# Attention degrees spread over the partitions by DMA instead of by TensorE, with the clears dealt out and every engine's order rewritten

## The reference, cut to what matters

```python
attn = softmax(causal(q @ k.T))                 # per head, 256 x 256
out  = attn @ v
adj  = clip(attn + eye(n), 0, 1)
deg  = adj.sum(-1, keepdims=True)
for l in range(2):
    h = feats @ gnn_w[l] + gnn_b[l]
    feats = gelu((adj @ h) / deg + feats)        # feats starts as v
out  = layer_norm((out + feats @ lin_w + lin_b) @ Wo)
```

## Time and profile before

| | us |
|---|---|
| median of 3 runs (lowest, highest) | 1038.27 (1037.43, 1043.19) |
| the profiled execution | 1036.57 |
| its span | 1034.8 |
| PE, PEld, DVE, ACT, POOL busy | 1010.2, 870.6, 823.1, 780.6, 504.1 |
| batches 0 to 15 on PE | about 12 to 862 |

### The profile page before, as it was taken

The page is one execution under the profiler, slowest core; times in us unless marked ns, Lnnn a source line. Parts: engine busy times, 40 slices in busy tenths (PEclk is TensorE's granted clock), DMA queues, the critical chain, the costliest instruction groups (busy, mean ns, idle before and its releaser), DMA issues.

```text
span 1034.8 us, 27841 instructions
## 1 busy us (share of the span) xinstructions
PE 1010.2 (98%) x8600; PEld 870.6 (84%) x8600; DVE 823.1 (80%) x3622; ACT 780.6 (75%) x2180; POOL 504.1 (49%) x668
## 2 busy tenths in 40 slices
PE   4999999999999999999999999999999999999997
PEld 3788888888888888888888888888888888999995
DVE  4858788888888888888888888898989796767554
ACT  3868787878787878787878787878787876656662
POOL 4524345454545454545464646454545452655443
PEclk9999999999999999999999999999999999999999
DMA  6991000000000000000000000000000021222227
GB/s 170 396 365 36 9 2 16 5 11 8 10 9 10 9 10 9 10 9 10 9 10 9 10 9 10 9 10 9 10 9 10 2 82 44 75 63 73 61 67 253
DMA packets 48964, 50.03 MB, mean 48 GB/s; under 512 B 20601, under 2 KB 39291, under 8 KB 48912
## 3 DMA queue, kind: packets, MB, share of 16 engines
q1 hardware_dynamic: 44592, 40.91, 12.9%
q0 software_dynamic: 4320, 8.47, 2.4%
HBM read 21.23 MB, written 28.58 MB: 48 GB/s over the span
## 4 chain that ended last, share of the span: by engine, by line
PE 92%; ACT 3%; SPq 2%; DMA 1%; DVE 1%; issue 1%; POOL 0%; POOLq 0%; DVEq 0%
PE bank L671 74%; PE bank L748 3%; PE bank L783 3%; PE bank L758 3%; PE bank L761 3%; PE bank L759 3%; PE bank L1040 2%; PE bank L1022 1%; PE bank L989 1%; ACT eb L1174 1%; DMA pairs<-zout,zin 1%; ACT ea L1174 0%; SPq L371 0%; DMA got<-pairs 0%; ACT gt L1144 0%
## 5 line engine op out<-in xcount | busy, mean ns | idle before, releaser
L1478 DVE TENSOR_REDUCE nmax<-bank 128x1 f32<-128x128 f32 (+1 forms) x512 | 148.1, 347 | 25.2 <-PE bank L671 25.2
L535 POOL TENSOR_TENSOR ea<-ea,wgt 128x256 f32<-128x256 f32 x128 | 78.6, 614 | 144.3 <-DVE wgt L1500 144.2
L544 POOL TENSOR_TENSOR deg<-den,rs 128x256 f32<-128x256 f32 x128 | 80.8, 636 | 123.3 <-DVE eb L1491 122.3
L537 POOL TENSOR_TENSOR eb<-eb,wgt 128x512 f32<-128x512 f32 x128 | 133.3, 1041 | 0.0
L1174 ACT ACTIVATE ea<-bank,nmax 128x128 f32<-128x128 f32 x256 | 97.9, 383 | 46.3 <-DVE nmax L1478 35.8
L1174 ACT ACTIVATE eb<-bank,nmax 128x256 f32<-128x256 f32 x256 | 125.8, 491 | 0.0
L1144 ACT ACTIVATE gt<-bank 128x512 f32<-128x512 f32 (+1 forms) x256 | 111.5, 490 | 15.1 <-PE bank L761 10.8
L1491 DVE SCALAR_TENSOR_TENSOR eb<-idw,ssum,eb 128x256 f32<-128x256 f32 x256 | 114.0, 481 | 0.0
L671 PE MATMUL bank<-qk 64*128 64x256 f32 (+1 forms) x1024 | 109.9, 341 | 0.0
L568 POOL DMA_INDIRECT pairs<-zout,zin x71 | 70.8, 997 | 78.7 <-DVE zout L1994 67.4
L671 PE MATMUL bank<-gt,vnat 128*64 128x256 f32 (+1 forms) x1024 | 101.1, 334 | 0.0
(11 more groups left out here) (241 smaller groups left out, 3025.8 us busy)
## 6 DMA issues: line engine op xcount, KB each, us to landing
slots<-gu_lo SPq DMA_DIRECT2D x33, 520.0 KB, 15.0
zin<-slots SPq DMA_DIRECT2D x71, 65.0 KB, 1.8
got<-pairs SPq DMA_DIRECT2D x8, 512.0 KB, 6.4
zin<-in_guT SPq DMA_DIRECT2D x14, 216.0 KB, 2.9
raw_gu<-in_guT SPq DMA_DIRECT2D x8, 352.0 KB, 3.0
out<-x_all SPq DMA_DIRECT2D x7, 256.0 KB, 3.5
pairs<-zout,zin POOLq DMA_INDIRECT x71, 2.4
dn<-in_downT SPq DMA_DIRECT2D x2, 512.0 KB, 15.5
```

Source lines behind the costliest of these rows:

```text
L535: nc.gpsimd.tensor_tensor(ea[:, s], ea[:, s], wgt[:, s, 0:2].unsqueeze(2).to_broadcast([P, 2, P]), ALU.mult)
L537: nc.gpsimd.tensor_tensor(eb[:, s], eb[:, s], wgt[:, s, 2:4].unsqueeze(2).to_broadcast([P, 2, 2 * P]), ALU.mult).then_inc(p_g.sem, 1)
L544: nc.gpsimd.tensor_tensor(deg[:, s], den[:, s, :].unsqueeze(2).to_broadcast([P, 4, DHEAD]), rs[:, s, :].unsqueeze(2).to_broadcast([P, 4, D ...
L1478: done = V.tensor_reduce(nmax[:, n % 3, i:i + 1], score_bank(n, a)[:, TILE_SCORES[t]], X, ALU.max, negate=True)
```

## The change

Degrees go over the partitions by way of DRAM: POOL writes 4 numbers per partition, SP writes them to a DRAM tensor degs as 2 x 256 in the order of tokens, waits for that write (w_kept), and reads them back with each head's row repeated on 64 partitions into deg_wide (4 slots), which raises w_deg.

```diff
-        deg = at("deg", [P, 3, 4, DHEAD])
+        deg = at("deg", [P, 3, 4])
+        deg_wide = at("deg_wide", [P, SPREADS, TOKENS])
...
-        s_deg = Signal(sem("s_deg"), PAIRS)
+        w_kept = [Signal(sem(f"w_kept{i}"), 16 * PAIRS // SPREADS) for i in range(SPREADS)]
+        w_deg = [Signal(sem(f"w_deg{i}"), 16 * PAIRS // SPREADS) for i in range(SPREADS)]
...
 
         def score_bank(n, a):
             return bank[SCORE_BANKS[n][a]][:, :]
@@ -387,10 +392,29 @@
 
 
             sp.wait_ge(k_consts, 1)
-            for r in range(0, SLOT_ROWS, CLEAR * P):
+            def clear(r):
                 sp.dma_start(slots[r:r + CLEAR * P, :].rearrange("(p r) d -> p (r d)", p=P),
                              zero[:, :]).then_inc(w_clear, 16)
 
+            def spread(b, n):
+                i = n % SPREADS
+                p_deg.wait(sp, b, n + 1)
+                sp.dma_start(degs[i].rearrange("a (t p) -> p (a t)", p=P), deg[:, n % 3, :],
+                             allow_slow_non_contiguous=True).then_inc(w_kept[i].sem, 16)
+                w_kept[i].wait(sp, b, 16 * (n // SPREADS + 1))
...
+                sp.dma_start(deg_wide[:, i, :],
+                             degs[i].unsqueeze(1).to_broadcast([2, DHEAD, TOKENS])).then_inc(w_deg[i].sem, 16)
+
+            to_clear = list(range(0, SLOT_ROWS, CLEAR * P))
+
+            def spread_and_clear(b, n):
+                spread(b, n)
+                now = CLEARS * (b * PAIRS + n)
+                for r in to_clear[now:now + CLEARS]:
+                    clear(r)
+
+            for n in range(PAIRS):
+                spread_and_clear(0, n)
 
             sp.wait_ge(k_low, 2)
             sp.wait_ge(k_vlow, 2)
@@ -406,9 +430,18 @@
                     w_part.sem, 16)
 
             part_load(1)
+            for n in range(PAIRS):
+                spread_and_clear(1, n)
+            for r in to_clear[2 * CLEARS * PAIRS:]:
...
+                clear(r)
             with sp.Fori(2, BATCHES - 1) as b:
-                p_low.wait(sp, b - 1, 0)
-                part_load(b)
+                for n in range(PAIRS):
+                    if n == PART_AT:
+                        p_low.wait(sp, b - 1, 0)
+                        part_load(b)
+                    spread(b, n)
+            for n in range(PAIRS):
+                spread(BATCHES - 1, n)
             for e in range(2, EXPERTS):
...
             def degrees(b, n):
 
                 s = n % 3
-                nc.gpsimd.tensor_tensor(deg[:, s], den[:, s, :].unsqueeze(2).to_broadcast([P, 4, DHEAD]),
-                                        rs[:, s, :].unsqueeze(2).to_broadcast([P, 4, DHEAD]),
+                nc.gpsimd.tensor_tensor(deg[:, s, :].rearrange("p (a t) -> p t a", t=TILES),
+                                        den[:, s, :].rearrange("p (t a) -> p t a", t=TILES),
+                                        rs[:, s, :].rearrange("p (t a) -> p t a", t=TILES),
                                         ALU.mult).then_inc(p_deg.sem, 1)
 
             def token_power(p, i):
...
             def attended(b, n):
 
                 d_d.wait(dve, b, n + 1)
-                V.tensor_tensor(aT[:, n, :], psum(DEG_AT[n], TOKENS), aT[:, n, :], ALU.mult).then_inc(d_a.sem, 1)
+                w_deg[n % SPREADS].wait(dve, b, 16 * (n // SPREADS + 1))
+                V.tensor_tensor(aT[:, n, :], deg_wide[:, n % SPREADS, :], aT[:, n, :], ALU.mult).then_inc(d_a.sem, 1)
```

PE's degrees and the table DEG_AT go, and ACT's mixed_values waits for d_d (the difference) instead of d_a. Waits on d_a come into POOL's order, ahead of degrees 3 to 7:

```diff
-                if routed is not None:
-                    a_qk.wait(pool, b, 2)
-                    gate_up_low(b - 1)
                 if after is not None:
                     deviation(b + 1, 0, 3)
-                d_e.wait(pool, b, 1)
+                if routed is not None:
+                    gate_up_low(b - 1)
+                graph(b, 0)
                 degrees(b, 0)
-                graph(b, 0)
                 graph(b, 1)
                 degrees(b, 1)
-                d_e.wait(pool, b, 3)
-                degrees(b, 2)
                 graph(b, 2)
-                d_e.wait(pool, b, 4)
-                degrees(b, 3)
-                graph(b, 3)
-                graph(b, 4)
-                graph(b, 5)
-                degrees(b, 4)
-                graph(b, 6)
-                degrees(b, 5)
                 if after is not None:
                     deviation(b + 1, 1, 7)
-                degrees(b, 6)
-                d_e.wait(pool, b, 8)
-                s_deg.wait(pool, b, 5)
-                degrees(b, 7)
-                graph(b, 7)
+                degrees(b, 2)
+                graph(b, 3)
+                d_a.wait(pool, b, 1)
+                degrees(b, 3)
+                graph(b, 4)
+                d_a.wait(pool, b, 2)
+                degrees(b, 4)
+                d_a.wait(pool, b, 3)
+                degrees(b, 5)
+                graph(b, 5)
+                graph(b, 6)
                 if before is not None:
                     token_power(b - 1, 0)
+                d_a.wait(pool, b, 4)
+                degrees(b, 6)
+                graph(b, 7)
+                d_a.wait(pool, b, 5)
+                degrees(b, 7)
                 if routed is not None:
-                    d_ch.wait(pool, b - 2, 11)
                     scatters(b - 2)
                 if before is not None:
                     token_power(b - 1, 1)
```

In scores the mask products of pairs 1, 3 and 6 (MASKS_LAST) come after the products of queries and keys instead of before them:

```diff
+                masks_last = n in MASKS_LAST
+
+                if not masks_last:
+                    masks()
                 for t in (1, 0):
                     for a in range(2):
                         rows = slice(a * DHEAD, (a + 1) * DHEAD)
                         mm = product(score_bank(n, a)[:, TILE_SCORES[t]], q[rows, xt(t)], k[rows, 0:(t + 1) * P],
-                                     False, True, skip_group_check=True)
+                                     masks_last and t == 1, not masks_last, skip_group_check=True)
+                if masks_last:
+                    mm = masks()
                 mm.then_inc(s_s.sem, 1)
```

More of the change, by code:

```diff
@@ L923, in batch @@
-                if before is None:
-                    folded_rest()
+                scores(b, 7)
+                layer2(b, 0)
+                differences(b, 4)
                 transposes(b, 5)
-                d_z1.wait(pe, b, 1)
-                degrees(b, 4)
-                if routed is not None:
-                    a_exp.wait(pe, b, 16)
-                    places(b - 2, psum(PLACES_AT, PLACES))
-                a_vt.wait(pe, b, 3)
-                layer1(b, 1)
-                if before is not None:
-                    output_natural(b - 1, psum(Y_NOW_AT, TOKENS))
+                if after is not None:
+                    a_exp.wait(pe, b, 15)
+                    queries_keys(b + 1, 0)
+                    d_z2.wait(pe, b, 1)
+                    values(b + 1, 0)
@@ L980, in batch @@
                 layer2(b, 3)
-                if before is not None and after is not None:
-                    a_qk.wait(pe, b + 1, 2)
                 if before is not None:
                     tokens_transposed(b - 1, psum(Z_T_AT, TOKENS))
+                output_graph(b, 0)
             def tokens_transposed(p, o):
@@ L1582, in batch @@
-                a_vt.wait(dve, b, 2)
-                difference(b, 2)
-                attended(b, 2)
-                maxima(b, 6, 0)
-                weights(b, 5)
-                maxima(b, 6, 1)
-                maxima(b, 7, 0)
-                difference(b, 3)
-                maxima(b, 7, 1)
-                attended(b, 3)
-                adjacency(b, 6)
-                weights(b, 6)
+                adjacency(b, 4)
+                difference(b, 2)
+                p_deg.wait(dve, b, 3)
@@ L1594, in batch @@
+                adjacency(b, 5)
+                if before is not None:
+                    output_bias(b - 1)
+                weights(b, 4)
+                attended(b, 1)
+                if before is None:
+                    folded_values()
+                difference(b, 3)
+                weights(b, 5)
                 layer1_out(b, 0)
                 if before is not None:
-                    output_bias(b - 1)
-                p_deg.wait(dve, b, 5)
-                adjacency(b, 7)
@@ L1610, in batch @@
                 if before is not None:
                     norm_tokens(b - 1, 0)
-                attended(b, 5)
-                if routed is not None:
-                    place_tokens(b - 2, 0)
+                layer1_out(b, 1)
+                p_deg.wait(dve, b, 4)
+                adjacency(b, 6)
+                attended(b, 2)
+                weights(b, 6)
+                attended(b, 3)
+                maxima(b, 7, 0)
+                maxima(b, 7, 1)
                 if before is not None:
@@ L1651, in batch @@
                     norm_tokens(b - 1, 8)
+                attended(b, 6)
+                if before is not None:
                     norm_tokens(b - 1, 9)
```

384 lines of the change are left out of this document (183 added, 201 removed).

## The result

The changed kernel takes 1729.95 us (median of 6 runs, 1727.47 to 1732.73) against 1038.41 (1036.56 to 1043.19): 1.666 times as long, 95% interval 1.664 to 1.669. The forecast was 1021. Its profiled span is 1725.7 us.

The account below looks back on a forecast made before the run. PE alone was taken to bound each batch: 16 batches x (1.6 - 0.3) = 20.8 us, less 6 at the end, 14.8 off 1036.57 gives 1021.8, called 1021; its own range 1011 to 1028, 8 in 10 1009 to 1034.

Parts of the forecast that it names:

- The sign: Whole kernel: forecast faster, with chance 0.77; within 0.5% 0.10, slower 0.15.
- The spread's time: Each pair's degree write to DRAM and read back: 3.9 to 5.9 us, taken as 5, hidden behind 8 us of DVE's order.
- the far row of 15: Spread's transfers: a queued transfer of 15 us, named as the other far row beside the 5 us taken.
- SP does not bound: SP's queue in each batch: held for 8 x 2.9 = 23 of 50.7 us plus its issues.
- Rival B: Loop: spread late, kernel slower; each microsecond over the cover of 8 paid twice per batch; 1054 at 9 us; 12%.
- the ring: Loop's cycle attended(n), degrees(n+3), write, read, attended(n+3): turns twice in a batch, with a cover of 8 us.
- The clears at 0: Batches 0 and 1: 33 writes of 520 KB, dealt out two behind each pair, costed at 0.
- PE's work and the new order: PE in each batch: 52.32 - 1.74 for removed transposes + 0.15 for the order's switches = 50.7 us.
- POOL's product: Degree product on POOL: shrinks from 128x256 at 0.61 us to 128x4 at near 0.19, freeing 3.4 us per batch.
- the stop in batch 15: End of last batch: PE stops behind ACT's gate_up_high(2), its up-weight loads queued behind the spread; 6 us once (3 to 9).
- Port collisions: DVE's attended, now with two SBUF inputs, blocked by POOL: one or two per batch, 0.5 to 1 us on DVE.
- the 0.3 of waits that the sum gave back: PE in each batch: 0.3 us for port collisions and the thin cover of transposes(5) together, bounds 0 and 1.

Follow-up runs that it names:

- best_sp: The same as best, but with the clears on SyncE's queue, two behind each spread of batches 0 and 1: 1086.07 us, ratio 1.044.
- best: Changed kernel with POOL's product ahead of graph, DVE's 32x32 turn, 128-byte write pieces, clears on POOL's queue, up-weight loads 2 to 4 among the last spreads: 1058.02 us.
- experiment 1: Changed kernel without the spread's write and read; deg_wide filled with ones once, true degrees left out: 1017.49 us, ratio 0.978.
- experiment 7: Changed kernel with the degree product moved from POOL to DVE, turned there in 32x32 blocks and written as 128 pieces of 128 bytes: 1130.05 us, ratio 1.088.

## Why the prediction was wrong

The sign was wrong by one term, and the size of the loss by a second and a third.

- **The spread's time** (the failed step). The sum had 2.1 to 2.9 us for the write and 1.8 to 3.0 for the read, from rows whose elements are as small or whose bytes are as many. Measured in the kernel: 8.8 for the write and 9.1 for the read with the next write behind it; by themselves 9.1 and 4.6. The text said that no four-byte write was in the trace, and still took the nearest rows as the bound. The four-byte row at 2.1 was a load into SBUF, and it says nothing on how a store into DRAM is acknowledged. The two together, forecast as 5, come to 18 us, over even the far row of 15 that it named.
- **"SP does not bound"** hung on that term: 8 x 2.9 = 23 of 50.7 us became 8 x 9.6 = 77. Rival B had the mechanism, at 12%, but its price let only the ring grow (1054). It ran out at a latency of 9 us, while SyncE's series, which it left at 23 us, alone reaches the batch's 50.7 at 50.7 / 8 = 6.3 us a pair. That check needed no new number. What no rival had is that the series doesn't overlap from batch to batch: the last read's landing and the steps behind attended(7) add 14 us, and 77 becomes 90.4.
- **The clears at 0** was wrong: 28 us between `best_sp` and `best`, and more that a second queue doesn't cure. The prediction placed two clears at 4 us behind each pair, but not that the next pair's write stands behind them in the same queue and SyncE behind it.
- **PE's work and the new order** were right: 50.7 forecast, 51.0 with what is given back, 50.93 measured. So were POOL's product (0.19 forecast, 0.202 measured) and the stop in batch 15 (6 forecast; 7.1 with the read, 3.5 without a transfer).
- **Port collisions**: none where attended stands close behind weights (128 of 128 within 0.425 us in experiment 1, with two SBUF inputs). Where the spread made it late, six of 128 ran into POOL's graph and took up to 1.28 us (mean of all 0.450), which was small change here. One or two a batch were forecast. PE is busy for all of the 50.9 us, so the 0.2 above 50.7 are its own work and not the 0.3 of waits that the sum gave back: two small errors nearly cancel there, and I have no row for the 0.2.
- **The clock** was in no rival. PE that waits also works more slowly: at 0.86 it was busy for 63.2 us with the work of 50.9.

## What to carry to other kernels

Before a transfer goes into a loop, time that very form (direction, element size, distance between neighbours) in a program of its own; the nearest row isn't a bound when the direction differs. Then hold two sums against the batch, not one: the latency against the cover, and the issuing queue's series (pairs x (wait + issues)), with everything else on that queue in it and with what must happen before the next batch's first transfer. A transfer that hides in the steady loop may not hide at the start and the end, where other transfers fill the queues; there the old way may stay.

## What the runs showed of the hardware

- 512 packed 4-byte stores into DRAM: packets done within 0.4 us, the engines' signals mostly 4 to 8 us later, 9.1 us in all; 128 pieces of 16 bytes in the same 2 KB take 1.9 us in all.
- A broadcast read of two 1 KB rows into 128 partitions takes 4.6 us from DRAM and 6.7 from SBUF; 128 different rows take 2.0. With a packed write right behind it the two take 9.4 to 11.4.
- DVE turned a 128x32 tile in 32x32 blocks in 0.20 us; by experiment 7's profile 0.21.
- The same loop body cost 2.4 us a turn more on DVE, and 3.6 us of the batch, in the kernels with 85 fetches against 25; by all that was seen, the place of the loop in the program decides it.
